# One order of stages for all engines, replaced by a written-out order for each

## What is computed

```python
x = x + 0.5 * ffn(layernorm(x))
x = x + attention(layernorm(x))
x = x + 0.5 * ffn(layernorm(x))      # the same weights
```

```python
def ffn(x):                                        # one adapter of N = 8 for a batch
    base = x @ W_base + b_base
    h = relu(x @ W_enc[n] + b_enc[n])              # for every n, 64 wide
    recon = h @ W_dec[n] + b_dec[n]
    n = argmin(mean((recon - x) ** 2))             # over rows and columns, per batch
    return base + relu(x @ W_down[n] + b_down[n]) @ W_up[n] + b_up[n]

def attention(x):                                  # 16 heads of 16
    q, k, v = rope(x @ Wq + bq), rope(x @ Wk + bk), x @ Wv + bv
    return softmax(q @ k.T / 4) @ v @ W0 + b0      # per head
```

## Time and profile before

| | |
|---|---|
| median of 3 runs | 1970.11 us (1966.84 to 1970.89) |
| profiled execution | 1970.23 us |
| its span | 1968.4 us |
| instructions | 26397 |
| mean granted clock of TensorE | 0.973 |
| TensorE, VectorE, ScalarE, GpSimd busy | 92, 65, 50, 26% |
| DMA | 99.40 MB, 50 GB/s on average |

### The profile page before, as it was taken

How to read it: one execution, slowest core, us unless ns; L and a number is a source line. 1 busy time by engine, 2 the same in 40 slices (tenths; PEclk the granted TensorE clock), 3 DMA queues, 4 the chain that set the end, 5 groups by cost and what they waited for, 6 DMA issues and landing times.

```text
span 1968.4 us, 26397 instructions
## 1 busy us (share of the span) xinstructions
PE 1812.3 (92%) x9128; PEld 988.0 (50%) x9128; DVE 1270.6 (65%) x2795; ACT 986.5 (50%) x1954; POOL 503.9 (26%) x663
## 2 busy tenths in 40 slices
...
GB/s 110 91 17 70 39 28 91 12 108 6 64 51 26 94 12 108 4 71 46 27 93 12 108 4 70 47 21 98 12 108 2 67 52 20 100 1 105 4 12 11
DMA packets 96781, 99.40 MB, mean 50 GB/s; under 512 B 19975, under 2 KB 88328, under 8 KB 96520
## 3 DMA queue, kind: packets, MB, share of 16 engines
...
...
## 4 chain that ended last, share of the span: by engine, by line
PE 61%; DVE 12%; DMA 12%; ACT 4%; SPq 4%; issue 4%; POOL 2%; POOLq 0%; ACTq 0%; DVEq 0%
PE ps L514 10%; PE ps L502 9%; PE ps L581 8%; PE ps L490 8%; DMA scratch<-parts 7%; DVE mx L832 6%; PE ps L560 6%; SPq L475 4%; PE ps L569 4%; DMA out_dram<-x 4%; PE ps L618 3%; PE ps L636 3%; ACT pr L716 2%; PE ps L621 2%; PE ps L681 2%
## 5 line engine op out<-in xcount | busy, mean ns | idle before, releaser
L832 DVE TENSOR_REDUCE mx<-ps 128x1 f32<-128x512 f32 x1024 | 653.5, 682 | 230.6 <-PE ps L490 229.6
L716 ACT ACTIVATE pr<-ps 128x512 f32<-128x512 f32 x1024 | 555.8, 598 | 292.0 <-PE ps L502 291.5
L490 PE MATMUL ps<-stack 96*128 96x512 bf16 x1024 | 326.1, 387 | 27.1 <-DVE mx L832 23.7
L502 PE MATMUL ps<-stack 98*128 98x512 bf16 x1024 | 323.2, 386 | 20.0 <-ACT pr L716 9.5
L514 PE MATMUL ps<-pr,va 128*32 128x512 f32 x2048 | 274.3, 608 | 4.6 <-ACT pr L716 4.6
L502 PEld LDWEIGHTS ps<-stack 98*128 98x128 bf16 x1024 | 77.5, 100 | 273.5 <-ACT pr L716 174.3
L771 ACT ACTIVATE h<-ps,benc 128x512 f32<-128x512 f32 x128 | 88.0, 687 | 216.2 <-PE ps L560 216.2
L490 PEld LDWEIGHTS ps<-stack 96*128 96x128 bf16 x1024 | 97.8, 98 | 187.8 <-DVE mx L832 91.7
L884 DVE SCALAR_TENSOR_TENSOR ps<-ps,wb,h 128x512 f32<-128x512 f32 x128 | 96.7, 755 | 140.7 <-PE ps L569 140.7
L1029 POOL TENSOR_SCALAR rs<-mv 128x4 f32<-128x4 f32 x48 | 11.6, 242 | 608.3 <-DVE mv L852 602.6
L581 PE MATMUL ps<-xh,w_dh 128*128 128x512 f32 x256 | 124.4, 486 | 9.2 <-DVE ps L884 6.7
(11 more groups left out here) (155 smaller groups left out, 2971.0 us busy)
## 6 DMA issues: line engine op xcount, KB each, us to landing
...
stack<-wu_mT SPq DMA_DIRECT2D x128, 4.0 KB, 1.7
...
```

Of the source, the lines that this page charges most:

```text
L490: pe.matmul(bank1[:, t % 2, :], stack[b.odd][0][0:KB, hd, 128 * t:128 * t + 128], stack[b.odd][1][0:KB, hd, :], start=True, stop=True).the ...
L502: pe.matmul(bank2[:, a % 2, :], stack[b.odd][1][:, 4 * g + a, 128 * t:128 * t + 128], stack[b.odd][0][:, 4 * g + a, :], start=True, stop=T ...
L716: act.activation(pr[:, n % 2, a, :], bank2[:, a % 2, :], ACT.Exp, scale=SCALE).then_inc(ex_done.sem, 1)
L832: dve.tensor_reduce(mx[:, hd // 4 % 2, e:e + 1], bank1[:, t % 2, :], AX.X, ALU.max).then_inc(mx_done.sem, 1)
```

## The change

`schedule`, `QK` and the step numbers go. In their place stand five functions, `tensor_order`, `scalar_order`, `vector_order`, `gpsimd_order` and `sync_order`, that list each engine's stages of one iteration, with the batch as an offset. The lists differ from engine to engine: an engine may meet two independent stages in another order than its neighbour. `walk` takes one of the lists.

```diff
-    for s in range(24):
-        for half in (0, 1):
-            if now:
-                if 5 <= s < 21: step("s2", i, s - 5, half)
-                if s < 16: step("s1", i, s, half)
-                if s in (3, 7, 11, 15) and half: step("ms", i, s // 4)
-                if 6 <= s < 22 and half == (s < 21): step("pv", i, s - 6)
-            dense(s, half)
+def walk(order, do):
+
+    for number in range(-2, B + 2):
+        def stage(name, ahead, *args):
+            b = Batch(number + ahead, number + ahead)
+            if 0 <= b.number < B and not (initial(b) and (name, *args) in BEGIN):
+                do[name](b, *args)
+
+        order(stage)
```

Beside the orders, four small edits. Two waits of TensorE are added for the bank `late`:

```diff
-                if s == 1 and c > 0 and not final(b):
-                    pe.wait_ge(*xT_done[1].at(b, c - 1))
+                if s == 1 and not final(b):
+                    pe.wait_ge(*(xT_done[1].at(b, c - 1) if c else mT_done.at(b + 1, 0)))
...
                 if p == 0:
                     pe.wait_ge(*h_done[f].at(b, NP - 1))
+                    if late_f:
+                        pe.wait_ge(*mT_done.at(b + 1, 2))
```

The sum over partitions for the cost is made into 32 rows and not 128, and `loss`, `tiny` and `adapter` shrink with it:

```diff
-        ones = va[:, 0, 0, HD:HD + 1].to_broadcast([128, 128])
+        ones = va[:, 0, 0, HD:HD + 1].to_broadcast([128, 32])
...
-                pe.matmul(bank[:, 0:N], ones, zt[f][:, 0, :], start=True, stop=False)
+                pe.matmul(bank[0:32, 0:N], ones, zt[f][:, 0, :], start=True, stop=False)
```

VectorE's `normalise` takes another form:

```diff
-                    dve.tensor_scalar(xn[s][:, t, 0:D], src[:, t, :], mv[s][:, t, 0:1], rs[s][:, t, :],
-                                      ALU.subtract, ALU.mult).then_inc(xn_done[s].sem, 1)
+                    dve.scalar_tensor_tensor(out=xn[s][:, t, 0:D], in0=src[:, t, :], scalar=mv[s][:, t, 0:1],
+                                             in1=rs[s][:, t, :].to_broadcast([128, D]), op0=ALU.subtract, op1=ALU.mult)\
+                        .then_inc(xn_done[s].sem, 1)
```

More of the change, by code:

```diff
@@ new lines, in vector_order @@
+def vector_order(stage):
+    stage("s1", 0, 0, 0)
+    stage("s1", 0, 0, 1)
+    stage("tl", +1, 0, 0)
+    stage("s1", 0, 1, 0)
+    stage("tl", +1, 0, 1)
+    stage("s1", 0, 1, 1)
+    stage("s1", 0, 2, 0)
+    stage("op", -1, 0)
+    stage("s1", 0, 2, 1)
+    stage("op", -1, 1)
+    stage("st", -1, 1, 0)
+    stage("st", -1, 1, 1)
+    stage("s1", 0, 3, 0)
+    stage("gr", +1, 0, 0, 1)
+    stage("s1", 0, 3, 1)
+    stage("ms", 0, 0)
+    stage("gr", +1, 0, 1, 1)
+    stage("s1", 0, 4, 0)
+    stage("gr", +1, 0, 2, 1)
+    stage("s1", 0, 4, 1)
+    stage("s1", 0, 5, 0)
+    stage("s1", 0, 5, 1)
+    stage("gr", +1, 0, 3, 1)
+    stage("s1", 0, 6, 0)
+    stage("s1", 0, 6, 1)
+    stage("cost", +1, 0)
+    stage("s1", 0, 7, 0)
+    stage("s1", 0, 7, 1)
+    stage("ms", 0, 1)
+    stage("s1", 0, 8, 0)
+    stage("pick", +1, 0)
+    stage("s1", 0, 8, 1)
+    stage("s1", 0, 9, 0)
+    stage("s1", 0, 9, 1)
+    stage("s1", 0, 10, 0)
+    stage("s1", 0, 10, 1)
+    stage("s1", 0, 11, 0)
+    stage("up", +1, 0, 0)
+    stage("s1", 0, 11, 1)
+    stage("ms", 0, 2)
+    stage("st", +1, 2, 0)
+    stage("up", +1, 0, 1)
+    stage("st", +1, 2, 1)
+    stage("s1", 0, 12, 0)
+    stage("lx", +1, 2, 0)
+    stage("s1", 0, 12, 1)
+    stage("lx", +1, 2, 1)
+    stage("s1", 0, 13, 0)
+    stage("gr", -1, 1, 0, 1)
+    stage("s1", 0, 13, 1)
+    stage("tl", +1, 2, 0)
+    stage("s1", 0, 14, 0)
+    stage("s1", 0, 14, 1)
+    stage("tl", +1, 2, 1)
+    stage("s1", 0, 15, 0)
+    stage("gr", -1, 1, 1, 1)
+    stage("s1", 0, 15, 1)
+    stage("ms", 0, 3)
+    stage("ro1", +1, 0)
+    stage("ro1", +1, 1)
+    stage("st", +2, 0, 0)
+    stage("gr", -1, 1, 2, 1)
+    stage("st", +2, 0, 1)
+    stage("ro3", +1, 0)
+    stage("lx", +2, 0, 0)
+    stage("lx", +2, 0, 1)
+    stage("gr", -1, 1, 3, 1)
+    stage("cost", -1, 1)
+    stage("pick", -1, 1)
+    stage("ro3", +1, 1)
+    stage("ro1", +1, 2)
+    stage("ro1", +1, 3)
+    stage("nt", 0, 0)
+    stage("nt", 0, 1)
+    stage("up", -1, 1, 0)
+    stage("nt", 0, 2)
+    stage("nt", 0, 3)
+    stage("up", -1, 1, 1)
+    stage("ro3", +1, 2)
+    stage("ro3", +1, 3)
+    stage("va", +1, 0)
+    stage("va", +1, 1)
@@ new lines, in gpsimd_order, with sync_order @@
+def gpsimd_order(stage):
+    stage("rs", -1, 1)
+    stage("tl", -1, 1, 0)
+    stage("tl", -1, 1, 1)
+    stage("zs", +1, 0)
+    stage("pick", +1, 0)
+    stage("zs", -1, 1)
+    stage("rs", +1, 2)
+    stage("b0", +1)
+    stage("ro1", +1, 0)
+    stage("ro2", +1, 0)
+    stage("ro1", +1, 1)
+    stage("rs", +2, 0)
+    stage("ro2", +1, 1)
+    stage("pick", -1, 1)
+    stage("ro1", +1, 2)
+    stage("ro2", +1, 2)
+    stage("ro1", +1, 3)
+    stage("ro2", +1, 3)
+def sync_order(stage):
+    stage("mt", 0, 1)
+    stage("mt", 0, 2)
+    stage("load", +2)
+    stage("mt", 0, 3)
+    stage("ro3", +1, 0)
+    stage("ro3", +1, 1)
+    stage("store", -1)
+    stage("ro3", +1, 2)
+    stage("mt", +1, 0)
+    stage("ro3", +1, 3)
```

429 lines of the change are left out of this document (264 added, 165 removed), and 3 rows, old and new, of the table QK.

## The result

| | before | after |
|---|---|---|
| median of 4 runs | 1970.5 us (1966.84 to 1977.59) | 1844.78 us (1842.78 to 1850.68) |
| ratio, 95% interval | | 0.9366 (0.9343 to 0.9388) |
| profiled execution, its span | 1970.23, 1968.4 us | 1844.28, 1842.5 us |
| mean granted clock | 0.973 | 0.982 |

Forecast were 1904 us and a range of 1862 to 1958. The direction was right and the gain is nearly twice the forecast one, 126 us for 66.

The account below looks back on a forecast made before the run. TensorE was taken as the bound, busy 92%, with 103.6 of 114.6 us a batch work. 4.2 a batch over 15 periods (63), 3 for batch 15 and 0.5 for the prologue, off 1970.2, gave 1904 us; range 1862 to 1958.

Parts of the forecast that it names:

- Tail: End of a batch, first qk to values: raw copied at once, nt starts 2.3 us sooner.
- Seam and head: Change of batches up to s2 0: first encode 2.9 us sooner, store wait gone, s2 0 5.0 won.
- the rest of the list: Signs it is right: no store or raw waits, ro3 ahead of the addition, s2 0 after 25 us, TensorE 94 to 95%.
- The walk wins 5.0 ... minus 0.8: Reordered tail, seam and head win 5.0 us a batch; some ten hand-overs take 0.8, leaving 4.2.
- Middle. ... I count zero: The 53 us of nearly pure TensorE work: 0.7 idle, about as much in stretched steps, no gain counted.
- The fear for `mt` 1 and 2: Middle: mt 1 and 2 have only 3.4 to 3.7 us to their s2, costing up to 0.3 each.
- 4.2 over 15 periods: Every batch period, batch 0 included, wins 4.2 us, 63 in all.
- 3: Batch 15, with no next batch, wins the copy of raw and two stalls, 3 us.
- Small edits: Cost in 32 rows for 128: 0.1 us a time at most; two-tensor normalise: +0.2 of VectorE a batch, hidden but 0.1.
- More than that: Rival: the middle's 1.5 us go too and hand-overs hide, 6 to 7 us a batch, 1860 to 1875; chance 0.16.
- Given back: Rival: the seam waits on GpSimd's chain, only 1.5 us a batch of the stalls arrive, 1946; chance 0.20.
- Slower: Rival: VectorE's lx waits for a late rs, passed one for one to TensorE; 4.5 late gives 1994; chance 0.10.

Follow-up runs that it names:

- a_raw: Changed kernel with ro2 of part 2 ahead of the last copy of raw on ScalarE, as before: 1861.42 us, ratio 0.9460 to the kernel before.
- b_raw: Kernel before with ro2 of part 2 moved behind the copy of raw on ScalarE, nothing else: 1981.18 us, ratio 1.0068.
- a_bunch: Changed kernel with the down product of the first ffn one step later on TensorE, leaving one pair of half heads bare: 1856.08 us.
- a_ts: Changed kernel with normalise in its old form, tensor_scalar: 1846.58 us.
- a_cost_pv: Changed kernel with the first ffn's cost three half steps later, directly ahead of pv 1 on TensorE and behind the maxima's split on VectorE: 1847.03 us.
- b_sp: Kernel before with the new order on SP alone, the store ahead of ro3 of part 2: 1946.74 us, ratio 0.9891.
- b_tail: Kernel before with SP's new order, raw copied first on ScalarE, and ro3 of part 2 behind nt and up on VectorE: 1929.13 us.
- a_undo: Changed kernel with eight pieces undone together (seam, raw, lx, one bare step, cost in 128 rows, normalise's form, whole Gram products, mt earlier): 1965.71 us.
- a_old_sp: Changed kernel with SP's old order, the store behind the round trip of part 2: 1847.89 us.
- a_cost128: Changed kernel with the cost made in 128 rows again, all orders kept: 1849.0 us.
- a_lx: Changed kernel with VectorE's lx of the next input back behind the last Gram product and the cost, ahead of the choice: 1852.71 us.
- a_raw_lx: Changed kernel with ro2 of part 2 ahead of raw on ScalarE and lx ahead of the choice on VectorE, both together: 1895.24 us.

## Why the prediction was too small

**Tail, right.** Counted from the first `qk` (1232.27 here, 1078.1 in the prediction's walk), forecast and measured: `rs` 13.1 and 13.3, `lx` 13.2 and 13.3, cost 17.1 and 17.0, choice done 19.2 and 18.7, last adapter row 22.0 and 21.4, `dn` 23.2 and 22.5, `nt` 24.7 and 24.0. The order of events is the forecast one. `lx` waited 1.25 for `rs`, which the prediction had named as a sign that it is wrong, and it wasn't: VectorE was only early. A wait's length says when the engine came, not that the work is late. a_raw prices the copy of `raw` at 1.3 a batch, b_raw shows that it needs VectorE's queue too: the change moves both, and the prediction names only ScalarE's.

**Seam and head, right.** The values' addition was forecast at 33.6 and came at 32.7, the first encode 40.5 and 40.0, `s2` 0 59.7 and 58.9. I had added 0.6 to GpSimd's chain for ScalarE's copy of `dn`; from last adapter row to the end of the last `rest` it took 9.7 us, as before. The rows confirm the rest of the list: no wait of `op` on the store, `ro3` directly ahead of the addition, `nt` without a wait for `raw`, `s2` 0 25.4 us after the first `s1`, TensorE 95% busy.

**The step that failed first: "The walk wins 5.0 ... minus 0.8".** The walk's stretch won 5.6, the steady gain of 7.44 less the middle's 1.8 (the starts above, 58.9 for 59.7, give 5.8). So no allowance for ten hand-overs was needed: they were inside the durations between starts that I had read, or hidden; which of the two no run tells. On record 4.2, measured 5.6: 1.4 a batch.

**The second: "Middle. ... I count zero".** It won 1.8 (48.35 us from `s2` 0 to `qk` 0, against 53.0 less the 1.8 and the 1.0 of work that the walk moves out of this stretch). I had read 0.7 of idle time there and as much in stretched steps, and priced moved half heads at nothing. The starts before and after show where it was: the bare pair took 0.8 more than its half heads cost (four half heads from 1161.57 to 1164.24, 2.67 us; a_bunch prices one at 0.65), the two `mt` 0.16 each and now 0.01, the first cost 0.47 and now 0.22, of which 128 rows in its new place would give back only 0.05. That is 1.35; the other 0.5 isn't taken apart. The fear for `mt` 1 and 2 was unfounded: `s2` behind them starts without a halt. 1.4 + 1.8 = 3.2 over 14 batches is 45 of the 59 us missed; the ends below are the rest. The prediction's own ceiling for an order, 7 us a batch from 103.6 of work and 4 that stay, was the better guide: the steady gain is 7.44, some 0.3 of it the cost.

**The third: the ends, "4.2 over 15 periods" for batch 0, and "3" for batch 15.** They gave 11.0 and 12.4. The clock is in both. In batch 0 TensorE was at half clock for 22 us before and 4 after; kernels with the new seam take 97.0 with 4 us of it and 99.4 to 100.0 with 12, so by this slope, an estimate, 5 to 6 of the 11.0 go with the clock. That the order causes the clock isn't shown: kernels that differ in a piece without effect there (a_ts, a_cost_pv) have 8 and 4 us. At the end most of the gain stands between the first `s2` and the first `nt` of batch 15, 72.0 us before and 64.7 after. Windows of before and then of after:

```profile
1833.41:1905.37 71.96, 67.00 (x313) 25.48 (x314) 33.78 (x66) 43.10 (x85) 5.15 (x11) 0.94 0.01 1
1715.51:1780.18 64.67, 62.31 (x310) 23.84 (x311) 34.10 (x68) 41.93 (x83) 5.16 (x11) 0.96 0.11 19
```

b_sp takes 72.2 there and b_tail 70.9, all kernels of the new order 64.6 to 66.9, so SP's order isn't it and the clock is little of it; a_undo's 66.9 says that the eight pieces aren't most of it either. Which places in the order are, I haven't taken apart. Up to that `s2` the end won another 4.4, with 6 us at half clock for 15, and b_sp 5.4, with 7; in the new order a_old_sp's end is no longer than a_ts's (151.0 and 151.5).

**Small edits.** The cost was forecast at 0.1 a time at most; a_cost128 gives 0.05 for the first and 0.2 for the second. `normalise` was put at 424 ns, from a form of the same size. Line 1114 in the changed kernel, durations min/median/max:

```profile
L1114 DVE SCALAR_TENSOR_TENSOR xn<-xin,mv,rs x64: 471/479/1389, 9.7 to 1568.7; 128x256 f32<-128x256 f32 x64
```

a_ts has 409 ns. So the new form costs 70 ns an instruction where 20 were forecast, and nothing in time. The speed factor that the Trainium skill gives a one-source fp32 form ("VectorE: DVE Perf Modes", section "Mode 2×_2P — use both read ports for one tensor") doesn't show in this pair either: 479 over 409 is 1.17.

**The rivals.** "More than that" was the right one of them: both its conditions came true, the middle's 1.5 (1.8) and hidden hand-overs. It was still short, by the ends and by 0.4 a batch. The argument against it, no slack behind GpSimd, fell with a_lx: 1.2 us. "Given back" fell with it. "Slower" had its mechanism right and its condition unmet: `rs` came in time. Its "one for one" holds only where `raw` stands behind `ro2` too (a_raw_lx); in the kernel as changed a late `lx` is paid at a third.
